# First layer's edge loop: the one-hot of each supertile built by ScalarE from distances instead of VectorE's compare

## The reference

```python
h = jnp.maximum(_layernorm(x, axis=-1), 0.0)
ei = jnp.concatenate([h[src], edge_attr], axis=-1)
core = jnp.maximum(ei @ W1 + b1, 0.0) @ W2 + b2
gate = jax.nn.sigmoid(ei @ Wg + bg)
agg = jax.ops.segment_sum(gate * core, dst, num_segments=N)
out = _layernorm(agg + h) * gamma + beta
x = x + out
```

## Time and profile before

| | |
|---|---|
| median of three runs | 3817.59 us (3802.13 to 3818.0) |
| profiled execution | 3809.7 us |
| its span | 3807.5 us |
| mean granted clock of TensorE | 0.968 |
| TensorE matmul busy | 3240.5 us (85%) |
| VectorE busy | 2582.1 us (68%) |
| ScalarE busy | 976.7 us (26%) |
| GpSimd busy | 2330.5 us (61%) |
| layer-0 loop | about 77 to 1421 us of the span |

### The profile page before, as it was taken

The page is one execution under the profiler, slowest core; times in us unless marked ns, Lnnn a source line. Parts: engine busy times, 40 slices in busy tenths (PEclk is TensorE's granted clock), DMA queues, the critical chain, the costliest instruction groups (busy, mean ns, idle before and its releaser), DMA issues.

```text
span 3807.5 us, 74477 instructions
## 1 busy us (share of the span) xinstructions
PE 3240.5 (85%) x21136; PEld 2775.7 (73%) x21137; DVE 2582.1 (68%) x3934; ACT 976.7 (26%) x1654; POOL 2330.5 (61%) x2362
## 2 busy tenths in 40 slices
PE   6999999999999987998777777777857778787776
PEld 4999999999999986886565566666645667665654
DVE  6999999999999988886676673333354444444444
ACT  3555555555555545441000000000010000000000
POOL 1666666666666640004776677777777777777775
PEclk8999999999999998999998999999989999999999
DMA  5666666666666643554555457555533333333333
GB/s 171 178 177 177 178 174 174 176 174 174 173 174 172 172 135 124 205 204 153 161 159 152 143 157 170 167 161 161 161 88 105 105 99 101 99 105 105 105 105 114
DMA packets 322744, 569.88 MB, mean 150 GB/s; under 512 B 73896, under 2 KB 218392, under 8 KB 322584
## 3 DMA queue, kind: packets, MB, share of 16 engines
q0 software_dynamic: 137984, 411.19, 38.2%
q1 hardware_dynamic: 182732, 154.33, 12.5%
q10 hardware_dynamic: 1868, 2.52, 0.2%
HBM read 452.43 MB, written 115.41 MB: 149 GB/s over the span
## 4 chain that ended last, share of the span: by engine, by line
PE 63%; DVE 16%; issue 11%; POOL 5%; DMA 3%; DVEq 2%; ACT 1%; POOLq 0%; ACTq 0%
PE pc L678 14%; PE pa L687 14%; PE pa L726 6%; PE pu L668 5%; POOL fa L423 5%; DVE tops L1220 5%; PE pg L652 5%; DVE key L1223 4%; PE pu L726 4%; PE pu L660 4%; PE pg L726 3%; DMA fa<-proj,gslot 2%; PE pu L784 2%; PE pg L784 1%; DVE onehot L1003 1%
## 5 line engine op out<-in xcount | busy, mean ns | idle before, releaser
L423 POOL DMA_INDIRECT fa<-proj,gslot x1568 | 1499.2, 956 | 884.9 <-issue 432.3
L406 POOL DMA_INDIRECT fa<-ptab,slot x784 | 827.4, 1055 | 542.6 <-issue 297.1
L687 PE MATMUL pa<-fa,onehot 128*128 128x258 f32 x1760 | 462.0, 410 | 219.4 <-DVE onehot L1003 147.4
L1003 DVE SCALAR_TENSOR_TENSOR fa<-pc,base,src_f 128x512 f32<-128x512 f32 x406 | 303.7, 751 | 449.6 <-PE pa L726 331.9
L678 PE MATMUL pc<-ws,hr 128*128 128x256 f32 x4704 | 597.2, 283 | 0.0
L687 PEld LDWEIGHTS pa<-fa,onehot 128*128 128x128 f32 x1760 | 342.9, 201 | 327.1 <-issue 275.3
L678 PEld LDWEIGHTS pc<-ws,hr 128*128 128x128 f32 x4704 | 563.8, 188 | 0.6 <-issue 0.6
L726 PE MATMUL pa<-fa 128*128 128x258 f32 x1568 | 373.8, 380 | 0.0
L726 PEld LDWEIGHTS pa<-fa 128*128 128x128 f32 x1568 | 297.3, 190 | 45.2
L726 PE MATMUL pu<-fa 128*128 128x258 f32 x784 | 199.7, 398 | 119.8 <-DVE acc L1060 71.3
L497 ACT CAST hr<-fa 128x1024 fp32r<-128x1024 f32 x196 | 206.6, 1054 | 317.8 <-DVE fa L1009 317.8
(11 more groups left out here) (151 smaller groups left out, 4782.4 us busy)
## 6 DMA issues: line engine op xcount, KB each, us to landing
proj<-fa SPq DMA_DIRECT2D x400, 256.0 KB, 2.3
fa<-in_ea_t SPq DMA_DIRECT2D x196, 128.0 KB
fa<-proj,gslot POOLq DMA_INDIRECT x1568, 2.8
fa<-ptab,slot POOLq DMA_INDIRECT x784
fa<-in_Wrel SPq DMA_DIRECT2D x32, 256.0 KB, 3.1
ptab<-fa SPq DMA_DIRECT2D x25, 256.0 KB, 2.0
out<-res SPq DMA_DIRECT2D x4, 768.0 KB
res<-in_x SPq DMA_DIRECT2D x1, 1792.0 KB, 20.5
```

Of the source, the lines that this page charges most:

```text
L406: pool.indirect_dma_start(pbuf[:, n % 2, j, :], None, ptab[:, :], bass.IndirectOffsetOnAxis(ap=slot[:, n, j:j + 1], axis=0)).then_inc(s_ga ...
L423: pool.indirect_dma_start(gbuf[:, n, j, 0:H], None, proj[k - 1][:, :], bass.IndirectOffsetOnAxis(ap=gslot[:, at, j:j + 1], axis=0)).then_i ...
L687: last = nc.tensor.matmul(pa[:, bank, 0:width], keys[:, at, j, :], rows[:, j, :], start=(n == 0), stop=(n == len(todo) - 1))
L1003: return nc.vector.scalar_tensor_tensor(out=(onehot0, onehot, onehot2[at // GS])[k][:, at % GS, :, :], in0=nodes, scalar=base[:, bass.ds(b ...
```

## The change

For each supertile ScalarE computes |node + 128 * first block - destination| for its four columns of 128 edges (four Abs activations, whose per-partition bias is a column of the new table `local`), and then Relu(1 - distance) over all 512, which is 1 where the two are equal and 0 elsewhere. The distances lie in part 0 of the tile `onehot`, which the first layer does not use otherwise; `local` lies in `srt`. `local` is made once by VectorE, before `edge_keys`. The call of `one_hot` in VectorE's loop goes; the compares for further blocks stay. ScalarE works on the one-hot of s-1 in the step of s.

```diff
+        local, dist = srt[:, :], onehot[:, 0, :, :]
...
+            def distances(s, j0):
+
+                if past(s, 1) and j0 == 0:
+                    act.wait_ge(s_oh[0], s)
+                for j in (j0, j0 + 1):
+                    last = nc.scalar.activation(dist[:, j, :], iota[:, :], ACT.Abs, bias=local[:, bass.ds(J * s + j, 1)])
+                if j0:
+                    last.then_inc(s_dist, 1)
+
+            def one_hot(s, par):
+                act.wait_ge(s_dist, s + 1)
+                if past(s, 2):
+                    act.wait_ge(s_agg[0], s - 1)
+                nc.scalar.activation(onehot0[:, par, :, :], dist, ACT.Relu, bias=1.0, scale=-1.0).then_inc(s_oh[0], 1)
...
                     if not (last and u == GS - 1):
                         features_high(GS * r + u + 1, 1 - u % 2, 2 * r + (u + 1) // 2)
+                    if first and u == 1:
+                        act.wait_ge(s_local, 1)
+                    if u or not first:
+                        distances(GS * r + u - 1, 0)
                     relu_high(GS * r + u, u % 2)
+                    if u or not first:
+                        distances(GS * r + u - 1, 2)
                     gates(GS * r + u, u % 2)
                     if u or not first:
+                        one_hot(GS * r + u - 1, 1 - u % 2)
                         messages_high(GS * r + u - 1, 1 - u % 2)
...
             l0_quad(ST // GS - 1, last=True)
+            for j in range(0, J, 2):
+                distances(ST - 1, j)
+            one_hot(ST - 1, 1)
             messages_high(ST - 1, 1)
...
             windows(0)
+            nc.vector.scalar_tensor_tensor(out=local.rearrange("p (s j) -> p s j", j=J),
+                                           in0=wall[0][:, 1, :].unsqueeze(2).to_broadcast([P, ST, J]), scalar=float(-P),
+                                           in1=dst_f[:, :].rearrange("p (s j) -> p s j", j=J),
+                                           op0=ALU.mult, op1=ALU.subtract).then_inc(s_local, 1)
             edge_keys()
...
             messages(0, 0)
-            one_hot(0, 0, 0, dst_f, windows_of(dve, 0, 0, 1)[0])
             messages_low(0, 0)
...
                     messages(2 * i - 1 + u, 1 - u)
-                    one_hot(0, 2 * i - 1 + u, 1 - u, dst_f, w[u + 2])
                     add_first(2 * i - 2 + u, u, w[u + 1])
                     messages_low(2 * i - 1 + u, 1 - u)
...
             messages(ST - 1, 1)
-            one_hot(0, ST - 1, 1, dst_f, w[2])
             add_first(ST - 2, 0, w[1])
             messages_low(ST - 1, 1)
```

More of the change, by code:

```diff
@@ L215, in gnn_program @@
         s_oh = [sem(f"s_oh{k}") for k in range(3)]
+        s_local = sem("s_local")
+        s_dist = sem("s_dist")
         s_agg = [sem(f"s_agg{k}") for k in range(3)]
```

## The result

| | before | after |
|---|---|---|
| median | 3810.48 us (20 runs; 3802.13 to 3818.0) | 3816.92 us (20 runs; 3811.36 to 3821.64) |
| profiled execution, span | 3809.7, 3807.5 us | 3817.31, 3815.5 us |

The ratio is 1.0017, with a 95% interval of 1.0011 to 1.0023: no change by the bound of 0.5%, but clear of 1, and 6.4 us against the +0.3 us of the prediction's sum. The prediction's own median of before was that of three runs; over twenty it is 3810.48.

A forecast was written before the change was run, and what follows sets the result against it. TensorE was taken to bound the first layer's loop; 0 in the stretch, +1.0 us at the start and -0.66 at the end gave +0.3 us on the median of 3817.59, so 3817.9 us, range 3799 to 3838.

The forecast's parts named there:

- the +0.3 us of the prediction's sum: Whole kernel: 0 in the loop's stretch, +1.0 us at its start, -0.66 us at its end.
- The bound: First layer's loop: TensorE sets the pace, busy 1307.20 of 1308.00 us; VectorE a near second at 92%.
- The compare is not on the path: First layer's loop: removing 145 us of VectorE's compares gains nothing, as VectorE then waits for ScalarE's cast.
- The predicted 150 us of idle time: VectorE before the low message part: some 0.75 us idle per supertile, about 150 us in all instead of 8.3.
- The price on ScalarE: First layer's loop: four Abs and one Relu add 2.26 us per supertile, 5.74 of 6.62 us, fitting ScalarE's idle time.
- rival A: First layer's loop: ScalarE becomes the bound, +0.23 us per supertile, +45 us, 3863 us; chance 0.07.
- The rule against: Trainium skill: relu belongs on VectorE; rows agree on engine time, 2.26 for 0.75 us, but put it in holes.
- The ends: First layer's loop: a new VectorE instruction costs +1.0 us at the start; a removed compare saves 0.66 us at the end.
- The second layer is untouched: Second layer: the change adds and removes no time there.

The follow-up runs named there:

- e4: Kernel before without the 196 compares and nothing in their place, with a never-run VectorE block as padding: ratio 0.9995 to before.
- e7: Changed kernel with eight Abs per supertile instead of four, the extra ones into a tile nobody reads: ratio 1.0014 to before.
- e5: Changed kernel with VectorE's compare kept beside the activations, into a tile nobody reads: median 3814.90 us, ratio 1.0011 to before.
- e2: Changed kernel with a never-run block of 37 VectorE instructions at the end of the first layer: 3805.17 us, ratio 0.9992 to before.
- e1: Changed kernel run again as it stands: 3816.68 us, ratio 1.0018 to before.
- e9: Changed kernel with the same never-run block of 37 VectorE instructions, placed behind the second layer's forward aggregation: ratio 1.0016 to before.

## Why the prediction was right, and where it was not

**The bound.** Right. TensorE stays at 99.9% and its pace with VectorE lighter (e4), with ScalarE fuller (e7), and with both at once (e5).

**The compare is not on the path.** Right, shown by e4. The predicted 150 us of idle time before the low part of the message were 132.7. The removed busy time was 125 us in the stretch and not 145: each of the 194 compares cost 0.65 us, since an instruction's recorded duration overlaps its neighbour's.

**The price on ScalarE.** The duration was right (0.41 us taken, 397 ns measured), the term was too large: 4 x 0.41 + 0.62 = 2.26 us was a sum of durations, and the engine's busy time rose by (1003.86 - 688.24)/194 = 1.63 us. Back-to-back activations overlap, a pair of Abs takes 0.69 us, and ScalarE's total came to 1296 and not 1420 us. (The prediction also took 6.62 us for every supertile; on the average of 6.74 ScalarE's load before is 688.24/194 = 3.55 us and not 3.48, which changes nothing in the argument.) The rival A, built on the same sum, was therefore further away than it seemed: the point at which ScalarE decides was put at 0.63 us for one Abs; eight Abs instead of four did not reach it, twelve did. The step that tells this is in the earlier trace rows already: two Relus in 1.09 us, each recorded at 597 ns. The prediction named it against rival A and left it out of its own sum.

**The rule against.** By the row, ScalarE pays 1.63 us for 0.65 us of VectorE. The rule of the Trainium skill (ScalarE: Activation LUTs, Rules for kernel authors) that relu and the like belong on VectorE is borne out as to the engine's time; as to the kernel's it decides nothing while both stay under TensorE's pace.

**The ends.** The start cost 0.83 us (89.24 to 90.07) against 1.0 predicted, and TensorE's wait for the second compare near the end fell by 0.59 us (2.11 to 1.52) against 0.66. But these two are not what the +0.3 us of the loop's end is made of. Of the 0.83 us only 0.18 are left at the last regular sum before that wait (L687 at 1406.77, L715 at 1406.95), and the further sum starts 0.42 us earlier than before (1409.58 against 1410.00). This gain is then lost on VectorE. L1128, which adds that sum, started at 1411.74, 0.97 us after TensorE was done (1409.58 + 1.19); its counterpart of before, at 1411.40, started after 0.21 us:

```profile
1411.74 0.42 DVE L1128 TENSOR_TENSOR acc<-acc,pa 128x256 f32 x1 [1.03 <-PE pa L715]
1412.08 3.35 DVE L1139 TENSOR_TENSOR res<-res,beta_b 128x3072 f32<-128x3072 f32 x1
...
1415.46 1.22 DVE L1037 TENSOR_TENSOR fa<-fa,pc 128x1024 f32<-128x1024 f32 x1
```

Behind it stands `add_beta` with 3.35 us, and the last message product begins when that has ended: 1415.46 against 1415.12 before, 0.34 us late; the last accumulation is then 0.3 us late. Why L1128 started late the rows don't name. The prediction had neither this chain nor the shrinking of the start's 0.83 us, so that its sum met the 0.3 us is luck.

**What was missed.** "The second layer is untouched" is the sentence that failed: its operations are, its time is not. Of the 8.0 us between the profiled spans, the loop has 0.3, the stretch up to the end of the forward aggregation 6.7 and the rest of the program 1.0. That the place of VectorE's code decides most of this is shown by e2 against e1 and e9; why this place is worse is not, nor what part TensorE's lower clock has in it. The 3817.9 us of the forecast stand close to the measured 3816.92 us partly by chance, since it was made from a median of before that was 7.1 us above the one of twenty runs.

## What to carry to other kernels

Read who waits last for a step before paying to move it: here one row, VectorE's 8.3 us wait for the cast with the cast itself ending just before, said that the freed 0.65 us would be idle time. Cost a chain on an engine by start-to-start times, not by the sum of recorded durations; on instructions of 0.3 to 0.7 us the difference decides what fits. And when a change moves the time by a few tenths of a per cent, compare the stages it does not touch: a block that never runs, placed ahead of such a stage and behind it, helps to tell code placement from work. Count the instructions in the built program before choosing the block's length: here the count was 19 off, and the test of a rule for the bad places was lost by it.

## What was not expected of the hardware

The same stretch through the forward aggregation took 1348 to 1356 us or 1359 to 1363 us, and the kernels fall into the two groups by where VectorE's instructions lie, with VectorE's idle time put down to issue at 70 to 75 or 79 to 82 us. An Abs of 397 ns costs 0.27 us of ScalarE's time in a row of them, and where the engine was never idle the same Abs was recorded at 493 ns and cost 0.26 us. And engines of this loop can be filled to 93% (ScalarE, e7) without any change in the pace of an in-order chain of five engines.
